# A recurrent layer on one core: output scaling on another engine, one block of small products instead of two, a state update left out, and one product issued later

## The reference, cut to what matters

```
q = silu(conv(x @ Wq));  k = silu(conv(x @ Wk)) * 128**-0.5;  v = silu(conv(x @ Wv))
alpha = sigmoid(x @ Wa + ba);  beta = sigmoid(x @ Wb + bb)
step(S, t):                                   # S is a 128 x 128 state for each sequence and head
    S = alpha*S - beta * outer(S k - v, k)
    o = S q
o = (o - mean(o)) * rsqrt(var(o) + 1e-5) * ln_w + ln_b        # over the 128 values of a head
out = (o * sigmoid(x @ Wg)) @ Wo
```

## Time and profile before

| | |
|---|---|
| median of three runs (range) | 3112.66 us (3108.64 to 3117.06) |
| the profiled execution, its own time | 3114.06 us |
| its span, first to last instruction | 3112.3 us |
| PE busy, share of the span | 3052.7 us, 98% |
| PE weight load | 2519.4 us, 81% |
| DVE | 2022.6 us, 65% |
| ACT | 1667.1 us, 54% |
| POOL | 1295.5 us, 42% |
| mean granted TensorE clock | 0.994 |

### The profile page before, as it was taken

One profiled execution on the slowest core, in us unless ns is written; L12 is line 12 of the kernel. 1 busy time (PEld: TensorE's weight loads), 2 busy tenths in 40 slices (PEclk: granted clock), 3 DMA queues, 4 the chain that ended last, 5 costly groups with the idle time before them and its releaser, 6 DMA issues. The chain is left out here.

```text
span 3112.3 us, 61811 instructions
## 1 busy us (share of the span) xinstructions
PE 3052.7 (98%) x23992; PEld 2519.4 (81%) x23992; DVE 2022.6 (65%) x3722; ACT 1667.1 (54%) x4043; POOL 1295.5 (42%) x2223
## 2 busy tenths in 40 slices
PE   8999989999999999999999899999999999999999
PEld 7888867888888888888888678788888888888887
DVE  6112267778877888877788543746666666666666
ACT  5221357878778887878777733443333333222222
POOL 2222335656556655556565444323333223222212
PEclk9999999999999999999999999999999999999999
DMA  2100111111111111111111164311001101000004
GB/s 93 31 21 28 65 60 42 46 56 54 54 42 49 49 56 56 53 46 46 56 52 49 46 190 150 104 31 31 27 31 43 36 31 31 21 21 28 25 16 162
DMA packets 130245, 165.72 MB, mean 53 GB/s; under 512 B 9936, under 2 KB 72144, under 8 KB 129920
## 3 DMA queue, kind: packets, MB, share of 16 engines
q1 hardware_dynamic: 120592, 144.49, 15.2%
q10 hardware_dynamic: 9296, 17.04, 1.5%
q0 software_dynamic: 64, 0.23, 0.0%
HBM read 127.91 MB, written 33.82 MB: 52 GB/s over the span
## 5 line engine op out<-in xcount | busy, mean ns | idle before, releaser
L1469 DVE SCALAR_TENSOR_TENSOR b_zt<-b_rx,b_cw,b_zt 128x512 f32<-128x512 f32 x576 | 461.7, 802 | 22.0 <-POOL b_rx L1678 3.1
L70 PE MATMUL bank<-b_XH,b_wh 128*128 128x512 f32 x1024 | 460.3, 450 | 8.3 <-ACT b_zt L1221 7.0
L72 PE MATMUL bank<-b_XH,b_wl 128*128 128x512 f32 x1024 | 403.7, 394 | 0.0
L71 PE MATMUL bank<-b_XL,b_wh 128*128 128x512 f32 x1024 | 402.6, 393 | 1.1 <-issue 1.1
L70 PE MATMUL bank<-b_XH,b_qh 128*128 128x512 f32 x1024 | 399.5, 390 | 1.4 <-DVE b_g L2622 1.4
L72 PE MATMUL bank<-b_XH,b_ql 128*128 128x512 f32 x1024 | 399.1, 390 | 0.0
L71 PE MATMUL bank<-b_XL,b_qh 128*128 128x512 f32 x1024 | 398.9, 390 | 0.0
L2732 POOL TENSOR_TENSOR b_QHL<-b_qhd,b_QHH 128x512 fp32r<-128x512 f32 x124 | 176.5, 1427 | 456.1 <-ACT b_QHH L2500 453.8
L1724 POOL TENSOR_TENSOR b_PR<-b_A,b_T 128x15 f32<-128x15 f32 (+7 forms) x480 | 178.8, 373 | 177.7 <-issue 142.9
L2500 ACT CAST b_QHH<-b_qhd 128x512 fp32r<-128x512 f32 x124 | 76.9, 623 | 295.4 <-PE bank L72 178.4
L72 PEld LDWEIGHTS bank<-b_XH,b_wl 128*128 128x128 f32 x1024 | 192.9, 188 | 44.8
(11 more groups left out here) (269 smaller groups left out, 7611.2 us busy)
## 6 DMA issues: line engine op xcount, KB each, us to landing
b_abc<-tmp_a SPq DMA_DIRECT2D x64, 256.0 KB, 3.4
b_gbc<-tmp_g SPq DMA_DIRECT2D x64, 256.0 KB, 3.8
tmp_og<-b_gg SPq DMA_DIRECT2D x64, 256.0 KB, 2.4
b_mo<-tmp_og SPq DMA_DIRECT2D x64, 256.0 KB, 3.2
b_wr<-in_Wk SPq DMA_DIRECT2D x16, 256.0 KB, 3.1
b_wr<-in_Wq SPq DMA_DIRECT2D x16, 256.0 KB, 4.2
b_wr<-in_Wv SPq DMA_DIRECT2D x16, 256.0 KB, 2.7
b_wr<-in_Wg SPq DMA_DIRECT2D x16, 256.0 KB, 4.1
```

The lines of the kernel that those rows point to most:

```text
L70: e.do.matmul(out, wh, xh, start=first and k == 0, stop=False)
L71: e.do.matmul(out, wh, xl, start=False, stop=False)
L72: m = e.do.matmul(out, wl, xh, start=False, stop=last and k == n - 1)
L1469: e.do.scalar_tensor_tensor(out=z[:, :], in0=rx[:, j:j + 512], scalar=cw[:, u // 2, KIND[name[0]], j:j + 1], in1=z[:, :], op0=ALU.mult, op ...
```

## The change

1. `scaled` goes from DVE to POOL, with the same eight instructions. On POOL it stands in the round `i` for unit `i - 3`, behind `tail(i - 1, "q1")` and on both sides of `ones`.
2. `inverse4` is one visit of eight blocks. It stands where the second visit was, and the projections that lay between the visits now lie ahead of it.
3. For the last chunk of a head (`ends(u, ch)`: odd unit, `ch == 3`) the key transposes, the scaled `KD`, the product `chain3` and the state update are left out, as nothing reads that state. The counts of the semaphores `kvc`, `ds` and `st` are worked out by `turned_parts` and `updates`. The first chunk of the next head waits for `ws` in place of `st`.
4. `scores(i - 1, 3)` stands behind `turn(i - 3, 0)` and one k-slice of a gate projection, and no longer ahead of them.

The diff, without the renamed waits of the same kind:

```diff
+def ends(u, ch):
+    return u % 2 == 1 and ch == 3
+def updates(steps):
+    return steps - steps // 8
+def turned_parts(u, g):
+    return 12 * u - 2 * (u // 2) + 3 * (g + 1) - (u % 2) * ((g + 1) // 2)
...
@@ PE turn_kv
         for x in range(2):
-            e.do.transpose(kb[:, x * 256:x * 256 + 128], KQA[:, u % 2, b, c0 + x, :], ident)
+            if not ends(u, c0 + x):
+                e.do.transpose(kb[:, x * 256:x * 256 + 128], KQA[:, u % 2, b, c0 + x, :], ident)
@@ PE chain1 and chain2
-        e.wait_ge("st", 2 * at)
+        e.wait_ge("st", 2 * updates(at))
...
-            e.wait_ge("kvc", 3 * (4 * u + 2) + 3)
-            e.wait_ge("st", 2 * at)
+            e.wait_ge("kvc", turned_parts(u, 2))
+            e.wait_ge("ws", at)
@@ PE and DVE chain3
-        if not live(u):
+        if not live(u) or ends(u, ch):
             return
@@ PE order
-        scores(i - 1, 3)
         turn(i - 3, 0)
         project(gate_unit(i), "g0", 2, 3)
+        scores(i - 1, 3)
         chain2(i - 2, 0)
...
         project(i, "q1", 1, 2)
-        inverse4(i - 1, 0, 4)
         project(i, "k1", 3, 4)
         project(i, "q1", 2, 3)
-        inverse4(i - 1, 4, 8)
+        inverse4(i - 1)
@@ ACT turned_kv
+            if ends(u, c0 + x):
+                continue
             e.do.activation(t[f"KD{u % 2}"][:, b, c0 + x, :], kb[:, x * 256:x * 256 + 128], ACT.Copy,
@@ DVE order
         chain1(i - 1, 0)
-        scaled(i - 2, 0)
         masked(i, 0)
...
         masked(i, 7)
-        scaled(i - 2, 1)
         gated(i - 2, 0)
@@ POOL order
         tail(i - 1, "q1")
+        scaled(i - 3, 0)
         ones(i - 1)
         cut_next("v", i - 1)
+        scaled(i - 3, 1)
         decayed_q(i - 1, 0)
```

More of the change, by code:

```diff
@@ L724, with emptied @@
 BEFORE = bank_befores()
+def emptied(n, u):
+    if n[:2] == "kv":
+        return "kvc", turned_parts(u, int(n[2]))
+    name, steps, step = EMPTIED[n]
+    return name, steps * u + step
 def bank_free(e, n, u):
@@ L731, in bank_free @@
     else:
-        other, unit = BEFORE[n, u]
-        name, steps, step = EMPTIED[other]
-        e.wait_ge(name, steps * unit + step)
+        e.wait_ge(*emptied(*BEFORE[n, u]))
 def bank_over(e, b):
     _, _, last = max((lag, i, n) for i, (n, lag, at) in enumerate(TURNS) if at == b)
-    name, steps, step = EMPTIED[last]
-    e.wait_ge(name, steps * (NU - 1) + step)
+    e.wait_ge(*emptied(last, NU - 1))
 def weight_of(p, h):
@@ L974, in inverse3, with inverse4 @@
         r.then_inc(S["s3"], 1)
-    def inverse4(u, m0, m1):
+    def inverse4(u):
         if not live(u):
@@ L980, in inverse4 @@
         kb = bank[BANK["s4a"]]
[L981 to L984, removed]
+        bank_free(e, "s4a", u)
+        e.wait_ge("zs", u + 1)
+        for m in range(8):
             for q in range(4):
@@ L990, in inverse4 @@
                 r = e.do.matmul(kb[qs, 256 + m * 32:288 + m * 32], MN[qs, 0, m, :], ZS[qs, m, :], start=True, stop=True)
-        if m1 == 8:
-            r.then_inc(S["s4"], 1)
+        r.then_inc(S["s4"], 1)
     def inverse5(u):
@@ L1079, in chain3 @@
         e.wait_ge("ws", at + 1)
-        e.wait_ge("kvc", 3 * (4 * u + 2 + ch // 2) + 3)
+        e.wait_ge("kvc", turned_parts(u, 2 + ch // 2))
         for b in range(2):
@@ L1246, in turned_kv @@
         e.wait_ge("kv", 4 * u + g + 1)
-        e.wait_ge("ds", 4 * (u - 2) + 4)
+        e.wait_ge("ds", updates(4 * (u - 2) + 4))
         sums_stored(e)
@@ L1341, in chain2 @@
         e.wait_ge("p2", at + 1)
-        e.wait_ge("ds", at - 1)
+        e.wait_ge("ds", updates(at - 1))
         sums_stored(e)
@@ L1548, in chain3 @@
     def chain3(u, ch):
-        if not live(u):
+        if not live(u) or ends(u, ch):
             return
         (at, n), (h, half) = chain_step(u, ch), divmod(u, 2)
-        e.wait_ge("ds", at + 1)
+        e.wait_ge("ds", updates(at + 1))
         e.wait_ge("p3", at + 1)
-        e.wait_ge("st", 2 * at)
+        e.wait_ge("st", 2 * updates(at))
         for b in range(2):
@@ L1574, in first_guess @@
         e.do.tensor_scalar(y.bitcast(I32), a.bitcast(I32), -1.0, float(0x5F3759DF), ALU.mult, ALU.add).then_inc(S["nr"], 1)
[L1576 to L1584, removed]
     def gated(u, b):
@@ L1750, in root, with scaled @@
         e.do.tensor_tensor(y, y, a, ALU.mult).then_inc(S["nw"], 1)
+    def scaled(u, b):
+        if not live(u):
+            return
+        e.wait_ge("nw", 12 * u + 12)
+        e.wait_ge("mu", u + 1)
+        for ch in range(4):
+            i = 4 * b + ch
+            r = e.do.tensor_scalar(t["OS"][:, b, ch, :], t["OS"][:, b, ch, :], ss[:, 4, i:i + 1], ss[:, 2, i:i + 1], ALU.subtract, ALU.mult)
+        r.then_inc(S["osc"], 1)
     def ahead(u, c0, c1):
@@ L1975, in mix0_act @@
     e.wait_ge("p3", 4 * NU)
-    e.wait_ge("ds", 4 * NU)
+    e.wait_ge("ds", updates(4 * NU))
     for n in range(4):
```

## The result

| | before | after |
|---|---|---|
| median of 11 runs on one chip (range) | 3112.66 us (3108.64 to 3117.06) | 3105.20 us (3103.53 to 3106.82) |
| ratio, 95% interval | | 0.9974 (0.9966 to 0.9983) |
| span of the profiled execution | 3112.3 us | 3103.8 us |

The account below looks back on a forecast made before the run. PE's issue was taken to bound the kernel at 98% busy. Terms −9.3 − 6.7 − 3.5 − 3.6 + 1.0 = −22.1 us from 3114.06 gave 3092.0; the median 1.4 lower, so 3091, range 3083 to 3105.

Parts of the forecast that it names:

- One visit, unread state, transposes: PE work removed: single `inverse4` visit −9.3 us, fifteen `chain3` −6.7 us, 32 key transposes −3.5 us.
- Rival A: At `inverse4`, the long run of small products pays nothing back: 3100, at the far bound 3108; chance 0.12.
- the price of `scaled` on POOL and its room: Each instruction 0.45 us on POOL, four 1.8 us against 3.1 us of room in even rounds; the move costs 0.
- Rival B: `scaled` on POOL somewhat late, 0.75 to 0.95 us each; even rounds wait, up to 19 us, half likely: 3100; chance 0.11.
- The waits at `turn`: PE's waits at `turn` on `masked` and scaled outputs go, −3.6 us; +1.0 put for smaller margin in odd rounds.
- work taken off PE is worth all it takes: Mid-layer premise: PE's issue binds, so removed PE work counts in full, and work off DVE, ACT or POOL nothing by itself.
- Nothing counted: End of the layer: the last turn waits for roots then `scaled`, one to two microseconds on either engine; no cost taken.
- The scans, issue and clock: Scans beside POOL may lengthen (within +1.0); no gain from 1.8 us issue waits; differing clock dips cost or give 3 to 7 us.

Follow-up runs that it names:

- e12: Changed kernel with cheaper `scaled` on POOL (constants for the first four, one scalar from memory for the second four; outputs not normalised properly): 3091.39 us, one run.
- e8: Kernel before with only the unread state and its key transposes left out: 3109.35 us, ratio 0.9987.
- e7: Kernel before with only the single visit of `inverse4`: 3116.14 us, ratio 1.0005.
- e14: e7 with the third of POOL's three root steps left out: 3099.17 us, ratio 0.9953.
- e2: Changed kernel with `scaled` back on DVE and the fourth scores back ahead of the first turn; single visit and unread state remain: 3106.53 us, ratio 0.9977.
- e6: e5 with the last unit's `scaled` back on DVE in its old places: 3086.98 us, ratio 0.9914.
- e5: Changed kernel with the first turn behind the last scores and all eight `scaled` on POOL ahead of a weight's low part: 3090.79 us, ratio 0.9926.
- e9: e2 with the third of POOL's three root steps left out: 3092.54 us, ratio 0.9936.
- e11: Changed kernel with `scaled` back on DVE in its old places and the first turn moved behind the last scores: 3105.41 us, ratio 0.9976.

## Why the prediction was wrong

- **One visit, unread state, transposes: right.** 0.34 for a unit where 0.30 was taken, 0.45 and 0.11 as taken. In PE's work that is −20.7 us where −19.5 was written. Rival A is out: the long run goes on at its pace.
- **The failed step is the price of `scaled` on POOL and its room.** The prediction took 0.45 us by a line through other forms, with 1.3 us to spare, and a cost of 0. It is 0.79, and 0.90 in the four that PE waits for. The limit, given as 0.77 or 0.74, is lower still, (2.75 − 0.15) / 4 = 0.65, with 1051.25 − 1047.49 − 3.61 = 0.15 us for the hand-over: I had moved PE's request by the scores' 0.86 but not by the 0.34 of the shorter visit. At e12's 0.66 (0.72 in the four that PE waits for, still over the limit) most of the time is back, which shows this step. Rival B named this place and size; its chance of 0.11 was too low, with a high bound of 0.80 just above the limit. It said 0.8 at the first turn and 0.4 at the second, and it is 1.0 and 0.
- **The waits at `turn` were to go (−3.6 us, +1.0 for odd rounds).** They grew from 8.0 to 19.0 us.
- **The premise "work taken off PE is worth all it takes" failed too.** It holds where PE's queue alone sets the pace, and for work that stands on the way itself (e8). In even rounds one wait of 0.23 was already there, so work removed between `inverse3` and the turn turns into wait. e7 shows it (−0.68 us of work for a pair, +0.10 of time), e14 that the work pays, in the main, once the way is shorter. So with a right price of `scaled` alone I would have put the loss to POOL, and e2 shows that without POOL it comes as well, from the same way.
- **"Nothing counted" for the end of the layer.** The two turns wait 5.15 + 2.35 = 7.5 us, where the same two waited 3.54 + 0.87 = 4.4 before: 3.1 us. e6's waits there are 2.7 us shorter than e5's, and its median is 3.8 lower, though the intervals of the two overlap.
- **The scans, issue and clock.** The mean granted clock is 0.994 in both profiled executions. The waits on issue are 3.7 us from 540 to 1655 us in both traces, as taken. DVE's scans beside POOL take 1.29 us where they take 0.41 alone, and `turn` waits for `masked` nowhere in the changed kernel's list.

GpSimd's price bears on one rule. The Trainium skill, "GPSIMD Engine Reference", section "Engine selection", gives one-input operations on GpSimd as roughly line rate. The trace disagrees: four take 3.61 us on POOL and 1.11 on DVE in e9, some three times as long; the page's main advice, VectorE for elementwise work, agrees better with it. Yet e5 against e11, 3090.8 and 3105.4, shows that here the dearer engine is the better place once it has room.

The causes of the single waits on issue stay open, and so does the part of e8's gain that is missing from its whole time.

## What to carry to other kernels

An engine that is 98% busy can still be bound by a latency in every second round: one short wait that comes back in each of them says so, and work removed beside that way is not gained, while work removed on it is. Before counting such work, measure from the product that starts the way to the one that waits for it, and count every instruction on that way, on all engines, against what PE has left beside it. Then look at what else the same removal brings closer, since a second wait may be right behind. Then move the waiting step later, or what delays the way behind it, in the same change as the savings.

## What the runs showed of the hardware

- A two-scalar instruction of 128x128 in f32 took 0.79 us on POOL (median), 0.65 with two constants, 0.61 with one scalar from memory, and 0.28 (1.11 / 4) on DVE.
- DVE's four took 2.28 us where they met a POOL instruction of 1.29, and 1.11 where they didn't; the scan 1.29 to 1.37 against 0.41. The Trainium skill, "SBUF — State Buffer", section "SBUF: two separate sides", has DVE and GpSimd share a port pair that one of them holds for a whole instruction. The 1.17 us agree with that better than with a shared rate.
- A wait of PE at `turn` cost 0.18 to 0.23 us more than its row shows, in all traces that have one there. Ahead of `inverse3`, idle time of 0.14 us cost 0.20.
- One visit of 128 small passes costs 1.42 us from edge to edge, two of 64 cost 1.76. Each change to 32x32 products and back is 0.34 us.
